# First attention of a four-layer net: norm as steps of the attention, heads loaded through DRAM

## The reference, cut to what matters

```
x = L0_attn_x                                  # (2, 1024, 256), float32
xn = _layernorm(x, axis=-1)                    # (x - mean) / sqrt(var + 1e-5)
x = x + _L0_attn_ref(xn, Wq, Wk, Wv, Wo) + _L0_ffn_ref(xn, w_gate_up, w_down)
...                                            # layers 1 to 3 likewise

def _L0_attn_ref(x, Wq, Wk, Wv, Wo):           # 16 heads of 16 features
    q = apply_rope(proj(Wq))                   # [x1*cos - x2*sin, x1*sin + x2*cos]
    k = apply_rope(proj(Wk))
    v = proj(Wv)
    scores = jnp.einsum('bhqd,bhkd->bhqk', q, k) / np.sqrt(HEAD_DIM)
    scores = jnp.where(causal[None, None], scores, -jnp.inf)
    out = jnp.einsum('bhqk,bhkd->bhqd', jax.nn.softmax(scores, axis=-1), v)
    ...                                        # heads side by side, times Wo
```

## Time and profile before

| | |
|---|---|
| median of 3 runs | 2914.04 us (2909.21 to 2926.05) |
| the profiled execution's own time | 2918.43 us |
| its span, first to last instruction | 2916.7 us |
| mean granted TensorE clock | 0.964 |
| PE busy over the span | 2744.7 us, 94% |
| DVE, ACT, POOL busy | 1664.5, 1070.1, 932.2 us |
| first `s1` product in PE | 62.58 us |

### The profile page before, as it was taken

One profiled execution on the slowest core, in us unless ns is written; L12 is line 12 of the kernel. 1 busy time (PEld: TensorE's weight loads), 2 busy tenths in 40 slices (PEclk: granted clock), 3 DMA queues, 4 the chain that ended last, 5 costly groups with the idle time before them and its releaser, 6 DMA issues. The chain is left out here.

```text
span 2916.7 us, 35158 instructions
## 1 busy us (share of the span) xinstructions
PE 2744.7 (94%) x13436; PEld 1712.6 (59%) x13436; DVE 1664.5 (57%) x3193; ACT 1070.1 (37%) x1952; POOL 932.2 (32%) x901
## 2 busy tenths in 40 slices
PE   5889989998999999999999998989999999979997
PEld 3556554655556556566565557646666666646665
DVE  4665672224665664755753325488888888743224
ACT  1445443112544533544543113334444344322222
POOL 3221210002322322322321005336666666641004
PEclk9999999997999999999999998889999999969998
DMA  4133131004000000000001000000000000061223
GB/s 130 30 52 57 20 58 59 0 1 142 1 1 0 1 1 1 1 1 1 1 15 64 37 1 29 1 19 14 14 15 12 16 15 13 9 268 55 66 66 100
DMA packets 53366, 100.64 MB, mean 35 GB/s; under 512 B 10128, under 2 KB 34832, under 8 KB 52048
## 3 DMA queue, kind: packets, MB, share of 16 engines
q1 hardware_dynamic: 49608, 88.94, 10.8%
q0 software_dynamic: 3072, 8.39, 0.9%
q10 hardware_dynamic: 520, 1.07, 0.3%
HBM read 54.32 MB, written 18.61 MB: 25 GB/s over the span
## 5 line engine op out<-in xcount | busy, mean ns | idle before, releaser
L1161 PE MATMUL ps<-back 128*128 128x512 f32 x576 | 292.0, 596 | 0.3 <-ACT back L1202 0.3
L1202 ACT ACTIVATE back<-ps 128x512 f32<-128x512 f32 x288 | 170.1, 597 | 266.2 <-PE ps L1152 264.5
L832 DVE TENSOR_REDUCE front<-ps 128x1 f32<-128x512 f32 (+3 forms) x384 | 195.5, 551 | 102.1 <-PE ps L686 76.8
L1197 ACT ACTIVATE back<-ps,front 128x128 f32<-128x128 f32 (+7 forms) x256 | 189.1, 739 | 77.0 <-DVE front L1242 75.2
L1152 PEld LDWEIGHTS ps<-front,back 128*128 128x128 f32 x1152 | 140.8, 141 | 118.6 <-issue 94.9
L1285 POOL TENSOR_TENSOR back<-back 128x512 f32<-128x512 f32 x72 | 91.5, 1270 | 359.6 <-DVE back L1230 359.5
L1295 POOL TENSOR_SCALAR back<-back,front 128x128 f32<-128x128 f32 (+5 forms) x192 | 142.7, 747 | 191.2 <-DVE front L1261 188.4
L791 ACT ACTIVATE back<-ps 128x1024 f32<-128x1024 f32 (+1 forms) x192 | 151.7, 811 | 130.8 <-PE ps L708 130.0
L1242 DVE TENSOR_REDUCE front<-ps 128x1 f32<-128x128 f32 (+7 forms) x256 | 194.0, 758 | 8.8
L1843 DVE TENSOR_TENSOR_SCAN back<-ps,back 128x512 f32<-128x512 f32 x128 | 155.6, 1216 | 44.2 <-PE ps L1660 44.2
L1152 PE MATMUL ps<-front,back 128*128 128x128 f32 x1152 | 170.5, 273 | 3.6 <-DVE back L1267 3.6
(11 more groups left out here) (306 smaller groups left out, 5792.7 us busy)
## 6 DMA issues: line engine op xcount, KB each, us to landing
whole<-l_w SPq DMA_DIRECT2D x32, 512.0 KB, 13.6
front<-back SPq DMA_DIRECT2D x128, 64.0 KB, 2.0
rounded<-rounded SPq DMA_DIRECT2D x120, 64.0 KB
rounded<-front SPq DMA_DIRECT2D x120, 64.0 KB
xg<-front SPq DMA_DIRECT2D x1, 6016.0 KB, 31.8
front<-xg SPq DMA_DIRECT2D x47, 128.0 KB, 2.1
yg<-front SPq DMA_DIRECT2D x47, 128.0 KB, 1.7
front<-l_win SPq DMA_DIRECT2D x1, 4640.0 KB, 17.6
```

Source lines behind the costliest of these rows:

```text
L832: e.tensor_reduce(self.nm[u % 2][:, r, t, h:h + 1], self.bank(step)[:, 0:n], AX.X, ALU.max, negate=True).then_inc(D.sem, 1)
L1161: e.matmul(PS[:, 7, :], self.V[:, j, G % 4 * 128:G % 4 * 128 + 128], self.turned(("turn", n, j)), start=(j == 0), stop=(j == qt)).then_inc ...
L1197: e.activation(self.P[n % 2][:, h, :nk], s[:, :nk], ACT.Exp, bias=st[:, 0, h:h + 1], scale=1.0, accum_out=st[:, 1, h:h + 1]).then_inc(A.se ...
L1202: e.activation(self.turned(step), self.bank(step), ACT.Copy).then_inc(A.sem, 1)
```

## The change

The norm is no longer a stage with a barrier behind it: its steps are put into the orders of `Heads0` (`nstats`, `nroot`, `nrows`, `nturn`, `nout`). Groups 0 and 1 of the norm (1024 tokens) come first, then `proj` of half 0, and groups 2 and 3 between and behind. `proj` runs by tokens first and by query and key second. ACT loads its square root table at the start (`warm`). The loads stand in SP's queue in the order `x` 0, query weights, `x` 1, key weights, tables, `x` 2 and 3, values and output, and each step waits for its own.

DVE clears (with ones) half of `KS`, POOL the other half; POOL clears `QS` and `V` only once 8 row blocks of the norm are scaled, and the second place of `QS` after half 0's `proj` steps.

High and low parts are written to two DRAM tensors, `qh` and `kh` (`keep`), and a head is read from there with two DMAs (`move`): for the queries 32 rows each written twice in turn, for the keys 32 rows and then the same 32 again. For set 0 the first 512 tokens are read ahead (`begun`), the others later. From set 2 on the DMA of two rows remains. All of it is issued by SP.

```diff
+        self.qh = nc.dram_tensor("qh", (4, 8, 2, 16, 1024), F32, kind="Internal").ap()
+        self.kh = nc.dram_tensor("kh", (4, 8, 16, 2, 1024), F32, kind="Internal").ap()
...
 class Zeros0(Stage):
     def dve(self, e, w):
-        e.memset(self.h.KS.bitcast(F32), 0.0).then_inc(self.blank.sem, 1)
+        e.memset(self.h.KS[:, 0].bitcast(F32), 1.0).then_inc(self.ks[0].sem, 1)
     def pool(self, e, w):
-        e.memset(h.V, 0.0)
+        e.memset(h.KS[:, 1].bitcast(F32), 1.0).then_inc(self.ks[1].sem, 1)
...
+        w.wait_ge(h.norm.xn, 8)
+        self.zeros(e, 0)
+        e.memset(h.V, 0.0).then_inc(self.done.sem, 1)
...
-        for i in range(4):
-            e.memset(h.KS[32 * i:32 * i + 2, :, i, :].bitcast(F32), 1.0)
...
     def order(self, engine):
-            for n, (x, tt) in enumerate((x, tt) for x in range(2) for tt in range(2)):
+            for n, (tt, x) in enumerate((tt, x) for tt in range(2) for x in range(2)):
...
+        early = {"pe": [(-4, "nturn", 0), (-3, "nturn", 1), (-1.41, "nturn", 2), (-1.04, "nturn", 3)],
...
     def pe(self, e, w):
-        w.wait_ge(self.load.arrived, self.load.total)
...
+                w.wait_ge(self.norm.out, 4 if k > 1 else tt + 1)
...
-    def move(self, e, w, z, h):
...
-        for i in range(4):
-            r = slice((64 if h < 2 else 0) + 16 * i, (64 if h < 2 else 0) + 16 * i + 16)
-            e.dma_start(q[r, :], (high[0], self.low[0])[i // 2][f, :]).then_inc(self.moved[s][h].sem, 16)
-            e.dma_start(k[r, :], (high[1], self.low[1])[i % 2][f, :]).then_inc(self.moved[s][h].sem, 16)
...
+    def keep(self, e, w, k, x, tt):
+        o = slice(tt * 512, tt * 512 + 512)
+        w.wait_ge(self.activations, self.an["proj", k, x, tt])
+        e.dma_start(self.half(k, x, 0)[..., o], self.high[x][:, o].bitcast(F32)).then_inc(self.kept[k][tt].sem, 16)
+        w.wait_ge(self.pooled, self.gn["proj", k, x, tt])
+        e.dma_start(self.half(k, x, 1)[..., o], self.low[x][:, o]).then_inc(self.kept[k][tt].sem, 16)
...
+    def rows(self, z, h, x, o):
+        i = 4 * (z % 2) + h
+        if x == 0:
+            return self.net.qh[z // 2, i, :, :, o].rearrange("a r t -> (a r) t").unsqueeze(1).broadcast_to(
+                [32, 2, o.stop - o.start])
+        return self.net.kh[z // 2, i, :, :, o].rearrange("r a t -> (r a) t").unsqueeze(0).broadcast_to(
+            [2, 32, o.stop - o.start])
...
+    def sp(self, e, w):
+        halves = [slice(0, 512), slice(512, 1024)]
+        self.keep(e, w, 0, 0, 0)
+        self.keep(e, w, 0, 1, 0)
+        self.keep(e, w, 0, 0, 1)
+        w.wait_ge(self.zeros.ks[0], 1)
+        w.wait_ge(self.zeros.qs[0], 1)
+        w.wait_ge(self.kept[0][0], 64)
+        for h in range(4):
+            self.move(e, w, 0, h, halves[0], self.begun[h])
+        self.keep(e, w, 0, 1, 1)
+        w.wait_ge(self.kept[0][1], 64)
+        for h in range(4):
+            self.move(e, w, 0, h, halves[1], self.moved[0][h])
...
```

More of the change, by code:

```diff
@@ L640, in wait_set, with wait_kept @@
         z = u // 2
[L641 to L647, removed]
+        if u == 0:
+            w.wait_ge(self.begun[h], 32)
+        else:
+            w.wait_ge(self.moved[z % 2][h], 32 + 48 * (z // 2))
+    def wait_kept(self, w, k):
+        if k > 0:
+            for tt in range(2):
+                w.wait_ge(self.kept[k - 1][tt], 64)
     def last(self, kind, u):
@@ L667, in pe @@
                 _, b, i = step
+                w.wait_ge(self.wv.arrived, self.wv.total)
+                w.wait_ge(self.norm.out, 4 if b > 0 else i // 4 + 1)
                 o = self.take(w, step)
@@ L704, in pe @@
                     w.wait_ge(self.activations, self.an["s2", u - 1, self.blocks(u - 1) - 1, a])
+                else:
+                    w.wait_ge(self.norm.out, 4)
                 w.wait_ge(self.activations, self.an["mt", u])
@@ new lines, in half, with move @@
+    def half(self, k, x, part):
+        return self.net.kh[k, :, :, part] if x else self.net.qh[k, :, part]
+    def rows(self, z, h, x, o):
[5 more added lines that the diff above has]
+            [2, 32, o.stop - o.start])
+    def move(self, e, w, z, h, o, signal):
+        s = z % 2
+        r = slice(64, 128) if h < 2 else slice(0, 64)
+        for x, t in ((0, self.QS), (1, self.KS)):
+            e.dma_start(t[r, s, h, o].bitcast(F32), self.rows(z, h, x, o)).then_inc(signal.sem, 16)
@@ new lines, in sp @@
+    def sp(self, e, w):
[12 more added lines that the diff above has]
+            self.move(e, w, 0, h, halves[1], self.moved[0][h])
+        w.wait_ge(self.zeros.ks[1], 1)
+        w.wait_ge(self.zeros.qs[1], 1)
+        for h in range(4):
+            self.move(e, w, 1, h, slice(0, 1024), self.moved[1][h])
+        for z in range(2, 8):
+            k, s = z // 2, z % 2
+            if s == 0:
+                for tt in range(2):
+                    for x in range(2):
+                        self.keep(e, w, k, x, tt)
+            for tt in range(2):
+                w.wait_ge(self.kept[k][tt], 64)
+            w.wait_ge(self.products, self.pn[self.last("s2", 2 * z - 3)])
+            for h in range(4):
+                self.move(e, w, z, h, slice(0, 1024), self.moved[s][h])
+                q = self.QS[:, s, h, :].bitcast(F32)
+                e.dma_start(q[32 * h:32 * h + 2, :], q[32 * h + 2:32 * h + 4, :]).then_inc(self.moved[s][h].sem, 16)
@@ L2741, in stages @@
 def stages(net):
-    start = Begin(net)
-    out = [start]
+    out = [Begin(net)]
+    x = [net.flag("x_in%d" % g, 16) for g in range(4)]
     h = Heads0(net)
+    zeros = Zeros0(net, h)
     Wgu, Wd = net.sb(WF0, 2, 2048), net.sb(WF0 + 4096, 8, 256)
     f = Load(net, "w_ffn", [(Wgu, "l0_wgu")], 1)
-    out += [h.load, f, Zeros0(net, h), Norm(net, work=h.work, x=start.x), Barrier(net)]
-    h.plan(net, f)
-    out += [h, Barrier(net)]
+    h.plan(net, f, Norm(net, work=h.work, x=x), zeros)
+    out += [Input(net, x, (0,)), h.wq, Input(net, x, (1,)), h.wk, h.wt, Input(net, x, (2, 3)), h.wv, f, zeros, h, Barrier(net)]
     beside = WK0 + 9728
```

149 lines of the change are left out of this document (75 added, 74 removed).

## The result

| | before | after |
|---|---|---|
| median, 20 runs each | 2916.14 us (2906.18 to 2926.05) | 2931.07 us (2919.4 to 2938.84) |
| the profiled execution's own time | 2918.43 us | 2920.76 us |
| its span | 2916.7 us | 2919.0 us |
| mean granted TensorE clock | 0.964 | 0.961 |
| first load of the stage behind the attention | 484.58 us | 495.66 us |

The ratio is 1.0048, with a 95% interval of 1.0036 to 1.006: the changed kernel is 15 us **slower**. 2898 was predicted, with a range from 2884 to 2908. The profiled execution of after is one of its fastest (2920.76 of 2919.4 to 2938.84), so the spans are no good measure of the difference. The last row of the table is: by it the attention ends 11.1 us later than before, and nothing behind it is changed.

A forecast was written before the change was run, and what follows sets the result against it. PE, busy 94%, can win only in the chain through the start to the first scores. 17.5 us ahead less 1 for key-read ends gives 16.5; 2918.4 less that, less 4.4 to the median, gives 2898 us, range 2884 to 2908.

The forecast's parts named there:

- Norm: Start: projections begin at 15.3 instead of 31.75, first scores come at 42.4, 20.2 us earlier.
- one of the prediction's own signs of being wrong: Listed as wrong: group 0's rows still taking 6 us, or first scores waiting for heads 0 to 3 over 2 us.
- DVE and POOL side by side: Norm's group 2 rows may meet POOL's adds, costing 4.7 us; PE needs them only at 30.8, so nothing counted.
- Two engines for a key read: Key reads, source repeat outermost: only two engines share one, 64 KB takes 2.45 us at 26.7 GB/s an engine.
- rival 4: First scores wait as before; the DRAM round trip takes 5 us more each leg than 2.1: 2908, chance 0.08.
- Rival 1: All 16 engines take part in the key reads: 26 us gained, 2888, chance 0.20.
- A read's fixed time: Reads from DRAM: 1.8 us fixed, from 2.1 for 128 KB less 0.3 for the bytes.
- The start: Up to unit 1's head 3: second tokens' heads at 56.0 to 64.2, kernel 17.5 us ahead from there.
- Clock: Half clock for the first 6 us or so behind the idle stretches, as before; counted 0, worth up to 2.
- Rival 2: Half clock lasts 27.5 us from 57 on, costing 8 us: 2906, chance 0.10.
- "Later sets": Sets from 2 on: a set takes 24.4 us against 25.2 before, so the 1.1 us of waits stay.
- Rival 3: Later sets' reads slow, 10.4 GB/s an engine, a set 52 us: about +57, 2971, chance 0.04.

The follow-up runs named there:

- Experiment 8: Changed kernel with keys written twice, half 0's last key writes before the first reads, and POOL's second QS clearing after all norm rows: 2890.16 us.
- experiment 1: Changed kernel with each head's keys read from DRAM by two reads of 32 rows, without a repeated source: 2889.49 us, ratio 0.9898 to the kernel before.
- experiment 6: Changed kernel with a later set's four two-row DMAs issued ahead of its eight reads: 2940.79 us, ratio 1.0068 to the kernel before.
- experiments 7 and 8: Changed kernel, keys written twice, half 0's last two key writes before the first reads: 2891.62 us; the second also delays POOL's clearing behind all norm rows: 2890.16 us.

## Why the prediction was wrong, step by step

The mechanism was the predicted one (two engines for a key read), and it was taken for the likeliest. What failed is what it does in the later sets, and at the start a read's fixed time was too small.

- **Norm: right, the first scores in part by luck.** Projections at 13.78 (15.3 predicted). Group 0's rows took 1.38, the table load (0.80 us in) is hidden. PE was done at 39.06, 3.3 us earlier than the 42.4 predicted (the projections took 13.90, not 15.49), and then waited 2.36 us for head 0: first scores at 41.42. A wait of more than 2 us there was one of the prediction's own signs of being wrong, and it came true.
- **DVE and POOL side by side: size off, harmless.** The prediction feared a meeting in group 2 (4.7 us). Group 2's rows, at 21.66, took 3.36 us beside POOL's adds, 2.0 more than alone; the larger meeting came in group 3, whose rows took 7.79 us, not 1.38, beside POOL's adds and memsets. PE got its last transposes 1.44 us late, in time for a read that landed at 41.4 anyway. Experiment 8 takes 3.5 us of it away and gains nothing.
- **Two engines for a key read: right.** Share 0.13, 47 to 51 GB/s over windows of 5 us, that is 24 to 25 an engine against the loads' 26.7. The reads of the second tokens began at 51.69 (51.1). First scores at 41.42 exclude rival 4, whose 5 us a leg no row gave; experiment 1 takes any slow road through the DRAM away: with all engines a set lands in 12 us. Rival 1 comes near the kernel without the repeat: 26 us faster than before, where experiment 1 measured 30 (2889.49 against 2919.47 on its chip). The Trainium skill (DMA: Bandwidth & Descriptors, Rules for kernel authors) holds by this; it also says there to put a dimension whose size is a multiple of 16 outermost. Both repairs do: the rows of a read are 32 in experiment 1 and 64 in experiment 2.
- **A read's fixed time: too small.** Head 0's key read was issued at 34.72, 2.7 us earlier than the 37.4 predicted, and landed at 41.4, after 6.7 us instead of 1.8 + 2.45. The agreement with the 41.7 predicted is luck. Experiment 1, where all engines share a read, has the part that is not bandwidth: the median from issue to landing is

```profile
rounded<-kh SPq DMA_DIRECT2D x16, 64.0 KB, 3.6
```

 against the 2.1 of the earlier trace rows for twice the bytes. In experiment 8 head 0 took 4.9 (35.37 to 40.23). What makes these reads slower than that row is not tested.
- **The start: 5 us too good.** Maxima at 54.20 (53.4), but the second tokens' heads at 58.02 to 69.16, not 56.0 to 64.2: the distance was 3.4 to 4.1 us, not 2.76, with reads of set 1 (256 KB each) queued behind from 56.28 on. So 12.5 us ahead at head 3, not 17.5.
- **Clock: counted 0, 1.7 lost, most of it elsewhere.** It was at 0.50 from 41 on rather than from 60, and came back at 75, 6 us behind the last wait, as forecast. Up to the next unit's maxima the lead shrank only from 12.5 to 12.3. PE waits for these maxima in both kernels, here in after and in before:

```profile
95.00:96.00 1.00, 0.00 (x0) 0.00 (x0) 0.86 (x3) 0.00 (x0) 0.47 (x1) 0.76 0.02 6
96.08 1.09 PE L708 MATMUL ps<-front,rounded 128*128 128x128 f32 x4 [2.17 <-DVE rounded L875]
...
107.00:110.00 3.00, 1.66 (x8) 1.18 (x9) 2.11 (x5) 0.99 (x2) 0.72 (x1) 1.00 0.01 3
108.34 0.63 PE L693 MATMUL ps<-front,rounded 128*128 128x128 f32 x4 [2.26 <-DVE rounded L848]
```

 In after the clock falls in this pause and stays at 0.50 to about 99; before it stayed up. By set 2's first issue the lead is 10.8, so about 1.4 of the 1.7 went here. Rival 2 (8 us) is out. Sets 2, 4 and 6 each lost some 2 more behind their waits, put down to half clock, which no step had.
- **"Later sets": the step that failed.** It read a set as 0.6 + 1.8 + 4 x 5.5 = 24.4 us against the 25.2 that it may take, "the same, so the 1.1 us of waits stay". Measured from 129.10 to 158.51: 29.4. Of the 5.0 more, 1.6 are the rate (at 25 GB/s an engine 256 KB on two take 5.24, with the queries' share 5.9, times 4: 23.6 for 22). The 2.4 of issue and fixed time were right here: the first bytes move 1.3 us behind the first issue, and PE begins about 1 behind the last bytes. So the other 3.4 lie within the transfers, 27 us where 23.6 are accounted for, and what fills them stays open: from 130 to 132 the share is 0.42 and 0.37, and at 136 to 138 it is down to nearly two engines' already (0.20 and 0.12), while SP's issue is held. The two-row DMAs between the reads are at most 0.8 of it (experiment 6).
- **No slack, so each us counts three times.** 29.4 - 25.2 = 4.2 late, and 4.7 to 5.0 waited in sets 2, 4 and 6; in sets 3 and 5 the place comes free earlier than the head is needed, and nothing is waited for. With the clock, 21.9 us in all, where the step had none. Rival 3 named just this place and its condition ("once a set takes more than the 25.2"), but priced it only at 10.4 GB/s an engine and gave it 0.04. (In that price no row gives the + 15 behind 139.91; with the sets begun 17.5 earlier, as the sum has it, it is about +25 and not +57.) It also put its gain-is-gone point at 30.7 a set; with half clock behind each wait, it is below 29.4.

The sum, from 2931 back: the start 5.0 less, the way from there to set 2 1.7, the later sets 21.9, together 28.6; less the 1 us that was taken off for the ends of the reads. That takes the predicted 16.5 ahead to 11.1 behind, as the table of sets has it. The other 4 of the 15 us between the medians stay unexplained; runs of one kernel differ by more than that.

Not settled: where the 3.4 us of a set go, why a first read takes 4 to 5 us even on all engines, and whether experiments 7 and 8 give anything: their runs lie 16 and 6 us apart, and the clock alone moves an end by 8 (experiment 8), so a us or two can't be told.

## What to carry to other kernels

A gap of 0.8 us between "needed" and "landed" is no slack when it rests on a rate read from another transfer: price a step also at a rate some per cent lower, times the number of places where it recurs, and give that case a chance of its own. Where a DMA repeats its source, look at which dimension is outermost: the same bytes as two plain reads, or written twice and read once, made 42 to 46 us of 2931 here. And when two halves of a change can be had apart, run them apart: one was worth -23 us, the other +22. Last, compare ends from single traces only where they differ by more than falls of the clock can make.

## What the runs showed of the hardware

- **Issues behind reads on few engines take longer.** SP's issues take 0.5 to 0.6 us, but 3.71 and 5.07 us behind the third and fourth key read of set 2, 3.7 to 5.1 at the same places of sets 3 to 7, and 3.53, 3.80 and 5.23 in set 1's, while for most of that time the share is that of two engines (0.12 from 137 to 138). It reads as if a queue were full, though no row shows the queue. In experiment 1 two issues of key reads take 1.05 together in most places and 2.81 at most. So a read on two engines also delays reads that would use more.
- **A pause of 2 us can end full clock, and need not.** PE was idle for 1.44 us up to 38.30, ended its transposes at 39.06 and was idle for 2.36 us before 41.42; the clock fell in the pause, at the end of the window 40 to 41:

```profile
38.00:40.00 2.00, 0.76 (x4) 0.40 (x4) 0.56 (x2) 0.90 (x1) 0.10 (x1) 1.00 0.52 149
40.00:41.00 1.00, 0.00 (x0) 0.00 (x0) 0.00 (x0) 0.12 (x1) 0.00 (x0) 0.95 0.13 49
...
42.00:44.00 2.00, 1.68 (x7) 1.28 (x6) 1.55 (x4) 0.00 (x0) 0.00 (x0) 0.50 0.72 267
...
74.00:76.00 2.00, 1.96 (x9) 1.47 (x9) 1.79 (x5) 0.81 (x1) 0.41 (x1) 0.74 0.30 100
```

 Before, the fall came in the fourth us of the idle time, and a pause of 2.26 us ahead of 108.34 left the clock at 1.00, where one of 2.17 ended it in after. In experiment 1, where PE waited 0.45 us for head 0, it stayed at 1.00 up to 50. So the length of the pause alone doesn't tell, and experiments 7 and 8 differ behind nearly the same work.
- **DVE's rows beside POOL's work** took 7.79 us for four blocks here and 6.08 before, 4.31 with the memsets kept away (experiment 8) and 1.38 alone. The Trainium skill (SBUF — State Buffer, Who interferes with whom) has a port pair that a scaling of this kind and a POOL instruction can hold against each other for the whole of an instruction; the rows agree with it, though none shows the ports themselves.
